# The last 512 tokens through all eight experts on chip, between the tiles ahead of a last list of 18 tiles

## The reference, cut to what matters

```python
x = L0_attn_X                                     # 16 x 512 x 128, float32
h = _layernorm(x) * (1 + ca) + sa
x = x + ga * mamba2(h)                            # d_inner 256, 4 heads, state 128, one scan over 512 tokens
h = _layernorm(x) * (1 + cb) + sb
# moe(h), 8192 tokens, 8 experts, top 2, hidden size 256
topv, topi = top_k(h @ Wg.T, 2)
comb = one_hot(topi) weighted by softmax(topv)    # tokens x 8
g, v = h @ W1[e].T + b1[e], h @ W2[e].T + b2[e]
eo[e] = (silu(g) * v) @ W3[e].T + b3[e]
x = x + gb * sum_e eo[e] * comb[:, e]
```

## Time and profile before

| what | us |
|---|---|
| three timed runs | 856.6, 860.14, 867.21 |
| median of the three | 860.14 |
| span of the profiled execution, first to last instruction | 851.0 |
| PE busy in it | 689.8 (81%) |
| DVE busy | 608.2 (71%) |
| POOL busy | 543.4 (64%) |
| ACT busy | 447.5 (53%) |

### The profile page before, as it was taken

One profiled execution on the slowest core, in us unless ns is written; L12 is line 12 of the kernel. 1 busy time (PEld: TensorE's weight loads), 2 busy tenths in 40 slices (PEclk: granted clock), 3 DMA queues, 4 the chain that ended last, 5 costly groups with the idle time before them and its releaser, 6 DMA issues. The chain is left out here.

```text
span 851.0 us, 13516 instructions
## 1 busy us (share of the span) xinstructions
PE 689.8 (81%) x3713; PEld 528.2 (62%) x3713; DVE 608.2 (71%) x1640; ACT 447.5 (53%) x967; POOL 543.4 (64%) x398
## 2 busy tenths in 40 slices
PE   3687897788788899979998999799993865577883
PEld 3255665567467677857786778567882744355662
DVE  2839969988987998999879987998673364122331
ACT  3665666565675677648755776376532321121230
POOL 1414333746547587867867788678678587537775
PEclk9798799798798999989989999899997798697997
DMA  5000001112114544554465345534755677757882
GB/s 185 12 1 0 1 26 38 50 51 63 44 49 123 137 117 95 135 129 111 95 162 117 91 112 113 145 69 112 175 132 126 169 174 163 169 130 149 202 180 26
DMA packets 81273, 88.85 MB, mean 104 GB/s; under 512 B 7360, under 2 KB 67696, under 8 KB 81200
## 3 DMA queue, kind: packets, MB, share of 16 engines
q1 hardware_dynamic: 54528, 61.37, 25.4%
q0 software_dynamic: 26672, 26.62, 17.4%
HBM read 54.50 MB, written 33.46 MB: 103 GB/s over the span
## 5 line engine op out<-in xcount | busy, mean ns | idle before, releaser
L466 POOL DMA_INDIRECT out<-xs x142 | 228.7, 1611 | 115.4 <-issue 53.3
L436 POOL DMA_INDIRECT rows<-payload,pos x128 | 133.3, 1041 | 46.4 <-issue 30.9
L884 DVE SCALAR_TENSOR_TENSOR xbc<-T,table,xbc 128x511 f32<-128x511 f32 (+2 forms) x192 | 141.7, 746 | 7.6 <-ACT xbc L616 3.0
L1459 PE MATMUL FX<-wt,hid 128*128 128x128 f32 x568 | 89.7, 305 | 19.6 <-DVE hid L1129 19.5
L658 ACT ACTIVATE sg<-FG,wt 128x256 f32<-128x256 f32 x142 | 59.3, 470 | 83.2 <-PE FG L1446 83.1
L1137 DVE SCALAR_TENSOR_TENSOR xs<-FX,xs 128x128 f32<-128x128 f32 x142 | 43.0, 344 | 80.7 <-PE FX L1459 80.7
L1459 PEld LDWEIGHTS FX<-wt,hid 128*128 128x128 f32 x568 | 75.3, 207 | 29.7 <-DVE hid L1129 22.5
L1446 PE MATMUL FV<-xt,wt 128*128 128x256 f32 x284 | 81.7, 414 | 12.6 <-DVE hid L1129 12.4
L1129 DVE SCALAR_TENSOR_TENSOR hid<-FV,wt,sg 128x256 f32<-128x256 f32 x142 | 61.9, 477 | 41.8 <-ACT sg L658 26.2
L665 ACT ACTIVATE xt<-FX 128x256 f32<-128x256 f32 x71 | 27.2, 382 | 116.2 <-PE FX L1436 114.4
L1446 PE MATMUL FG<-xt,wt 128*128 128x256 f32 x284 | 78.7, 402 | 6.6 <-DMA wt<-in_wt 6.0
(11 more groups left out here) (207 smaller groups left out, 1397.8 us busy)
## 6 DMA issues: line engine op xcount, KB each, us to landing
wt<-in_wt SPq DMA_DIRECT2D x71, 386.0 KB, 4.4
xs<-rows SPq DMA_DIRECT2D x71, 258.0 KB, 3.6
x<-in_x SPq DMA_DIRECT2D x8, 512.0 KB, 3.8
out<-x SPq DMA_DIRECT2D x8, 512.0 KB, 3.7
out<-xs POOLq DMA_INDIRECT x142, 4.1
rows<-pad SPq DMA_DIRECT2D x8, 258.0 KB, 4.1
rows<-payload,pos POOLq DMA_INDIRECT x128
gate_a<-gates SPq DMA_DIRECT2D x8, 128.0 KB, 4.2
```

Source lines behind the costliest of these rows:

```text
L436: pool.indirect_dma_start(d["rows"], bass.IndirectOffsetOnAxis(ap=pos[:, k, n:n + 1], axis=0), payload[:, n, :], None).then_inc(scattered, 16)
L466: pool.indirect_dma_start(d["out"], bass.IndirectOffsetOnAxis(ap=xs[:, t % XSR, c, PAY - 1:PAY].bitcast(U32), axis=0), xs[:, t % XSR, c, 0 ...
L884: last = nc.vector.scalar_tensor_tensor(out=xbc[:, t, k, tap:L], in0=T[:, k, 0:L - tap], scalar=w, in1=xbc[:, t, k, tap:L], op0=ALU.mult, ...
L1459: last = nc.tensor.matmul(FX[:, TR + c * D:TR + (c + 1) * D], hid[:, t % 2, f, c * P:(c + 1) * P], wt[:, t % WR, DOWN + f * D:DOWN + (f + ...
```

## The change

The last sequence (512 tokens, blocks 4 to 7 of pair 7) is no longer routed into `rows`. Its `h2` stays on chip, all eight weight sets are loaded once (five into the buffer `mda`, three into `decay`, both free after the mamba stages), and each of the 8 experts works on two pieces of 256 tokens: 16 dense units. DVE sums them up in `acc`, weighted with each token's share (0 for experts it did not choose), multiplies with the gate, adds x and SP stores that sequence (`store_dense`). NTILES falls from 71 to 67 and LAST from 22 to 18; tiles 49 to 66 are the last list. Pair 7 has 8 scatters, not 16.

A list UNITS gives the order of tiles (T) and dense units (D): T0 to T41, then D D T42, D D T43, D D T44, D D T45, D D T46, D T47, D T48, D D D D T49, T50 to T66: 42 units from T41 on, where there were 30 tiles. The loop ends after pass 7, and a tail follows it. In it, from T42 on, `expert_turn` writes bank YB and `expert_down` alternates between FX and YA; turns run three units ahead. `ranks(7)` stands behind `expert_up(T41)` on PE, `new_tiles(7)` behind `expert_out(T41)` on DVE. On SP the dense weights stand before and behind `store_x1(7)`, the zero rows between `load_rows(46)` and `load_rows(47)`.

```diff
-NTILES = NP * PT + LAG
+DT = L // TR
+NTILES = NP * PT - L * 2 // TR + LAG
...
+JS = J // 2
+ND = E * DT
+OPEN = PT * (NP - 2) - LAG
+AHEAD = 3
+EA = C * 2 * NH * P // WT
+def units():
+    seq, n = [("tile", t) for t in range(OPEN + 1)], 0
+    for t in range(OPEN + 1, NTILES):
+        for n in range(n, min(n + (2 if t < NTILES - LAST - 2 else 1 if t < NTILES - LAST else ND), ND)):
+            seq.append(("dense", n))
+            n += 1
+        seq.append(("tile", t))
+    return seq
...
             def store_x1(p):
                 sp_.wait_ge(x1_ready, p + 1)
+                if p < NP - 1:
...
+                else:
+                    sp_.dma_start(ov[:, 2 * p, :, :], x[:, p % XR, 0:JS, :]).then_inc(x1_stored, 16)
+            def load_dense_weights(part):
+                if part == 0:
+                    sp_.wait_ge(seg_psum, J * NP)
+                else:
+                    sp_.wait_ge(ya_psum, C * NP)
+                for e in (range(EA), range(EA, E))[part]:
+                    sp_.dma_start(wd[e], d["wt"][e, :, :]).then_inc(wd_in[part], 16)
...
+                if i == NP:
+                    set_pads()
...
+                if i == NP - 1:
+                    load_dense_weights(0)
                 if is_pair(i):
                     store_x1(i)
+                if i == NP - 1:
+                    load_dense_weights(1)
...
+            add_out(PT * NP - 27)
+            scatter(NP - 2, 7)
+            add_out(PT * NP - 26)
+            add_out(PT * NP - 25)
+            for q in (0, 1):
+                scatter(NP - 1, q)
+            add_out(PT * NP - 24)
+            second_weight(NP - 1)
+            for q in (4, 5):
+                scatter(NP - 1, q)
+            for t in range(PT * NP - 23, NTILES):
+                add_out(t)
...
+            def dense_shares():
...
+            def expert_out(u):
...
+                    got = (FX, YA)[u > OPEN and u % 2][:, TR + c * D:TR + (c + 1) * D]
...
+                        else:
+                            last = nc.vector.scalar_tensor_tensor(out=acc[:, j, :], in0=got, scalar=share[:, 0, j, e:e + 1],
+                                                                  in1=acc[:, j, :], op0=ALU.mult, op1=ALU.add)
...
+            expert_hidden(OPEN)
+            dense_shares()
+            for u in range(OPEN, len(UNITS)):
+                if u + 1 < len(UNITS):
+                    expert_hidden(u + 1)
+                expert_out(u)
+                if u == OPEN:
+                    new_tiles(NP - 1)
+                if UNITS[u] == ("dense", ND - 1):
+                    dense_result()
...
+            expert_turn(OPEN)
+            expert_down(OPEN - 1)
+            expert_up(OPEN, 0)
+            expert_up(OPEN, 1)
+            ranks(NP - 1)
+            for u in range(OPEN, len(UNITS)):
+                if u + 1 < len(UNITS):
+                    expert_up(u + 1, 0)
+                    expert_up(u + 1, 1)
+                if u + AHEAD < len(UNITS) and UNITS[u + AHEAD][0] == "tile":
+                    expert_turn(UNITS[u + AHEAD][1])
+                expert_down(u)
```

More of the change, by code:

```diff
@@ L50 @@
 LAST = NTILES - (PT * (NP - 1) - LAG)
+JS = J // 2
[11 more added lines that the diff above has]
+    return seq
+UNITS = units()
+UNIT_OF = {v: u for u, (k, v) in enumerate(UNITS) if k == "tile"}
 TABLE = (("ident", P), ("upto", P), ("after", P), ("before", P), ("expo", J), ("experts", E), ("conv_w", NCT * KC),
@@ L195, in program @@
         wout = mda[:, 0, 0:2, :]
+        flat_a, flat_b = mda[:, :, :, :].rearrange("p c n t -> p (c n t)"), decay[:, :, :, :, :].rearrange("p c k h t -> p (c k h t)")
+        wd = [flat_a[:, e * WT:(e + 1) * WT] if e < EA else flat_b[:, (e - EA) * WT:(e - EA + 1) * WT] for e in range(E)]
+        acc = xn[:, 0:JS, :]
         wmod = mda[:, 1, 0:6, :]
@@ L259, in landed, with unit, all_scattered, wait_dense @@
                 eng.wait_ge(added[t % 2], 32 * (t // 2 + 1))
+        def unit(t):
+            return UNIT_OF[t]
+        def all_scattered(p):
+            return 16 * 2 * (J * p - (JS if p == NP else 0))
         def pair_of_tile(t):
             return min((t + LAG) // PT, NP - 1)
+        def wait_dense(eng, n):
+            part = int(n // DT >= EA)
+            eng.wait_ge(wd_in[part], 16 * (EA, E - EA)[part])
         block = ctx.enter_context(nc.Block())
@@ L679, in _ @@
             modulations()
-            for i in range(-2, 13):
+            for i in range(-2, NP):
                 if is_tile(PT * i - 24):
@@ L1078, in split_b3 @@
             def split_b3():
+                nc.vector.tensor_scalar(sel_e[:, :], experts[0:BR, :], part["b3_expert"][0:BR, :], None, ALU.is_equal)
                 vec.wait_ge(b3_in, 16)
@@ L1122, in new_tiles @@
                                                    op0=ALU.mult, op1=ALU.add).then_inc(turns_ready, 1)
[L1124 to L1127, removed]
+            def dense_shares():
+                vec.wait_ge(tanh_ready, NP)
+                for k, sign in ((0, 0.5), (1, -0.5)):
+                    last = nc.vector.tensor_scalar(topf[:, k, JS:J], tanh[:, JS:J], sign, 0.5, ALU.mult, ALU.add)
+                link(last)
+                for k in range(2):
+                    last = nc.vector.tensor_tensor(out=share[:, k, :, :], in0=hot[:, k, JS:J, :], in1=wide(topf[:, k, JS:J], E), op=ALU.mult)
+                link(last)
+                link(nc.vector.tensor_tensor(out=share[:, 0, :, :], in0=share[:, 0, :, :], in1=share[:, 1, :, :], op=ALU.add))
@@ L1128, in expert_hidden @@
+            def expert_hidden(u):
+                kind, n = UNITS[u]
+                vec.wait_ge(sg_ready, u + 1)
+                vec.wait_ge(uv_psum, u + 1)
+                wait(vec, o_psum, u - 1)
+                w = wt[:, n % WR, :] if kind == "tile" else wd[n // DT]
                 for f in range(FT):
[L1129 to L1131 removed]
+                    last = nc.vector.scalar_tensor_tensor(out=hid[:, u % 2, f, :], in0=FV[:, f * TR:(f + 1) * TR],
+                                                          scalar=w[:, B12 + FT + f:B12 + FT + f + 1],
+                                                          in1=sg[:, u % 2, f * TR:(f + 1) * TR], op0=ALU.add, op1=ALU.mult)
@@ new lines, in dense_result @@
+            def dense_result():
+                p = NP - 1
+                vec.wait_ge(gate_b_in[p % 2], 16 * (p // 2 + 1))
+                vec.wait_ge(ro_ready, UNITS.index(("dense", ND - 1)) + 1)
+                link(nc.vector.tensor_tensor(out=acc, in0=acc, in1=gate_b[:, p % 2, 1, :].unsqueeze(1).to_broadcast([P, JS, D]), op=ALU.mult))
+                vec.wait_ge(xn2_ready, NP)
+                nc.vector.tensor_tensor(out=x[:, p % XR, JS:J, :], in0=x[:, p % XR, JS:J, :], in1=acc, op=ALU.add).then_inc(dense_out, 1)
@@ L1440, in expert_up @@
[L1440 to L1443, removed]
+                back[name] = (xt_ready, t + 1)
+            def expert_up(u, v):
+                kind, n = UNITS[u]
+                if kind == "tile":
+                    pe.wait_ge(wt_in[n % WR], 16 * (n // WR + 1))
+                    pe.wait_ge(xt_ready, n + 1)
+                    w, src = wt[:, n % WR, :], xt[:, n % 2, :]
+                else:
+                    wait_dense(pe, n)
+                    pe.wait_ge(h2_ready, NP)
+                    w, src = wd[n // DT], h2[:, L + n % DT * TR:L + (n % DT + 1) * TR]
+                wait(pe, (sg_ready, hid_ready)[v], u)
@@ L1461, in expert_down @@
                 last.then_inc(o_psum, 1)
-                back["FX"] = (ro_ready, t + 1)
-            for i in range(-2, 13):
+                back[name] = (ro_ready, u + 1)
+            for i in range(-2, NP):
                 if is_pair(i):
@@ L1606, in _ @@
                     to_tokens(i + 1, 3)
+            expert_turn(OPEN - 1)
+            turn_norm2(NP - 1)
+            expert_down(OPEN - 3)
+            expert_up(OPEN - 2, 1)
+            logits(NP - 1)
+            expert_down(OPEN - 2)
+            expert_up(OPEN - 1, 0)
+            expert_up(OPEN - 1, 1)
+            turn_h2(NP - 1)
+            expert_turn(OPEN)
[3 more added lines that the diff above has]
+            ranks(NP - 1)
+            for u in range(OPEN, len(UNITS)):
+                if u + 1 < len(UNITS):
+                    expert_up(u + 1, 0)
+                    expert_up(u + 1, 1)
+                if u + AHEAD < len(UNITS) and UNITS[u + AHEAD][0] == "tile":
+                    expert_turn(UNITS[u + AHEAD][1])
+                expert_down(u)
 def kernel(**inputs):
```

130 lines of the change are left out of this document (90 added, 40 removed).

## The result

The changed kernel takes 879.59 us in the median of four runs, the kernel before 863.67 in the four beside it. One run of the changed kernel, 887.95, was a slow one; the fast three have a median of 876.14, and the ratio, 1.0187 with a 95% interval of 1.0097 to 1.0278, is one of fast runs. It is slower, but the interval lies on both sides of 2%, so between the prediction's "slower" (0.42) and "the same" (0.51) the runs don't decide. On the chip of the second set of experiments it was 1.0204 (1.0164 to 1.0245). The prediction was 875 (858 to 888), 1.7% slower.

The account below looks back on a forecast made before the run. No engine is full, so waits decide; the end is POOL's chain of adds. Tile 49 at 771, plus list 86.8, plus 7.8 behind it gives span 865.6; with the same outside part (9.1) 874.7 us, range 858 to 888.

Parts of the forecast that it names:

- The count of strict steps: Last list, POOL: tiles whose add awaits the previous tile's landing (clashes no spare slot parts): seven of 17, before three of 21.
- The start of tile 49: First add of tile 49 on POOL, after PE's dense units: at 771 us (765 to 779).
- The list: POOL's adds from first of tile 49 to first of 66: 86.8 us, five strict steps at 7.5, two late, ten free.
- the two late ones: Strict steps to tiles 63 and 65 in the last list, with loads over: 6.0 us each, 12 together.
- the ten free ones: Last-list steps that need not wait for the previous tile's landing: 3.73 us each, 37.3 together.
- Behind the last add: From the first add of the last tile to the kernel's end: 7.8 us.
- the outside part: Time around the profiled span, taken as the 9.1 us between the earlier span and the median of its runs.
- 46.7 us of dense work is the price: PE, 16 dense units at 2.92 us, all ahead of tile 49: the cost paid for losing four tiles and a gap.
- The rival of the dense weight loads: Dense weight loads delay landings, `residual(7)` and rows, PE slower at 3.2 a unit: time 890 us; chance 0.11.
- the moved ranks: `ranks(7)` put behind the up of tile 41 on PE: that up could start up to 2.6 us earlier.
- Cheap strict steps: Rival: all strict steps of the last list at 6.0 us, start at 766, time 862, no change; chance 0.15.
- Free landings: Rival: landings cost nothing, every last-list step is issue-bound at 3.71 us, time 845, faster; chance 0.06.

Follow-up runs that it names:

- the second set of experiments: Later runs on one chip: the changed kernel again, ratio 1.0204 to the kernel before, and three edited kernels.
- e2: Changed kernel with four slots more in the last list (22 again, NTILES 71), dense units kept; ratio to the kernel before 1.0326.
- e1: Changed kernel with dense units one before each of tiles 43 to 56 (two before 42), dense store at SP's end; ratio to the kernel before 1.0008.
- e5: e1 with SP issuing, from tile 50 on, weights of tile t ahead of rows of tile t + 2; ratio to the kernel before 0.9964.

## Why the prediction was right

*The count of strict steps* was the core, and held in the changed kernel: seven, at the tiles named, and three in e2. It holds where PE is ahead of POOL; with dense units in the list (e1) eleven steps were long. *The start of tile 49*: 774.4 for 771. The up of tile 41 came at 675.88 for 678, PE went on at 698.58 for 699.8. Then the stretch was slower than reckoned: 3.03 start to start for a dense unit (709.28 to 712.31) where I had 2.92, 0.11 x 22 = 2.4 us, and behind the gap PE was at half clock until about 705 (the up of T42 took 2.05 for 1.03), 3 us and more for my 2. *The list*: 92.0 for 86.8. The five strict steps under load were 8.04 in the mean for 7.5, 2.7 us together; the two late ones 5.98 for 6.0; the ten free ones 39.8 for 37.3. *Behind the last add* 8.0 for 7.8. In all a span of 874.4 for 865.6, within the bounds of its terms.

*The step that failed* is the outside part: "with the same outside part, 874.7". I took 9.1 us as what lies around a span; it is 1.7. The rest was that the profiled execution of before was a quick one. The two errors, 8.8 too short a span and 7.4 too long an outside, nearly cancelled, and that 875 lies so near the 876.14 of the profiled run is luck to that extent. As a difference the forecast was 14.6 us; the medians say 15.9, but the two spans, which the sum was about, differ by 23.4. I also read too little where I wrote that PE is busy 19 to 21 of 25 us from pass 8 on: that is true of the windows shown, but in the four from 650 to 750 it was 12.4 to 18.5.

*"46.7 us of dense work is the price"* was too simple. In the order of e1 the whole change costs nothing that the runs can tell; what was paid is that the dense work stood ahead of the list, where POOL waited for it, instead of filling PE's idle time in the list. The rival of the dense weight loads had a little in it: `residual(7)` moved by 1.1 us, and PE waited 1.55 us for the weights of tile 39 where it was 0.47, but the moved ranks made up for that, as I had set it. Cheap strict steps exist, but in another order: 6.3 in e1 up to tile 49, where PE's 6.27 a tile would hardly have let them be shorter, and 8.0 in the changed kernel. Free landings are out.

## What to carry to other kernels

Where read-modify-write transfers follow one another, count the steps that wait for the predecessor's landing, not the tiles: taking four slots off a list left 92.0 of 94.4 us, because the spares that parted the clashes went with them. Work that needs none of the bound resource belongs beside the part that is bound by it, not ahead of it; with the same 16 units the kernel was 2% slower in one order and no slower in the other. Look, too, at what then sets the pace: in e1 and e5 it was PE for a part of the list, so there was little left to fill. And take the time around a span from a run that gives both, not from a profile of one execution and a median of others.

## What the runs showed of the hardware

The landing of the same 64 KB indirect add, read off strict steps from the start of the second issue (the step less 1.86 us for the first), took 4.1 us where no loads ran (tiles 63, 65), 4.0 to 5.6 in e1 up to tile 51, at a DMA share of 0.50 to 0.62, and 7.1 and 6.0 in the changed kernel (tiles 50, 51) at 0.67. The mean share doesn't tell these apart; I did not find out what does. The Trainium skill (DMA: Bandwidth & Descriptors, Anatomy of one DMA) has 2.0 us plus bytes/436e3, 2.15 us here; all the landings read off here lie above that. The two issues of a tile took 3.71 to 3.74 us in the last lists wherever nothing else held POOL up, also at a DMA share of 0.94.
